# A fused vision tower on one core: two expert tiles gathered by products with tables of ones and zeros, and fillers in the gaps of a solve

## The reference, cut to what matters

```python
scores = jnp.einsum('bsh,he->bse', x, wr) + br
expert_id = jnp.argmax(scores, axis=-1)
h = jax.nn.gelu(jnp.einsum('bsh,ehf->ebsf', x, w1) + b1[:, None, None, :], approximate=False)
y = jnp.einsum('ebsf,efh->ebsh', h, w2) + b2[:, None, None, :]
out = jnp.einsum('ebsh,bse->bsh', y, jax.nn.one_hot(expert_id, E, dtype=x.dtype))
```

## Time and profile before

| | |
|---|---|
| median of 3 runs | 687.46 us (687.45 to 689.64) |
| the profiled execution | 688.33 us, of which the span from first to last instruction is 686.5 |
| TensorE busy | 636.0 us (93% of the span) |
| VectorE, ScalarE, GpSimd busy | 318.3, 278.5, 152.9 us |
| mean granted TensorE clock | 0.968 of full speed |
| the chain that ended last | 77% of the span on TensorE, 13% on VectorE |

### The profile page before, as it was taken

The page is one execution under the profiler, slowest core; times in us unless marked ns, Lnnn a source line. Parts: engine busy times, 40 slices in busy tenths (PEclk is TensorE's granted clock), DMA queues, the critical chain, the costliest instruction groups (busy, mean ns, idle before and its releaser), DMA issues.

```text
span 686.5 us, 20153 instructions
## 1 busy us (share of the span) xinstructions
PE 636.0 (93%) x9158; PEld 467.7 (68%) x9158; DVE 318.3 (46%) x493; ACT 278.5 (41%) x558; POOL 152.9 (22%) x143
## 2 busy tenths in 40 slices
PE   8989879969999995999999988899999999999997
PEld 5646766859999993655665557554999866555553
DVE  0397456510111003757777786599247824311311
ACT  0486441303323231546666652857444532111223
POOL 9400110040111113324554464300333100000000
PEclk9999889889999998999999997999999999999999
DMA  9610045033889912010010201000000160000001
GB/s 320 204 66 4 3 188 205 1 97 114 334 311 315 339 62 75 0 33 23 26 33 23 83 6 62 3 1 0 4 5 4 45 266 1 0 0 1 0 1 47
DMA packets 19700, 56.69 MB, mean 83 GB/s; under 512 B 4079, under 2 KB 12383, under 8 KB 15263
## 3 DMA queue, kind: packets, MB, share of 16 engines
q1 hardware_dynamic: 18559, 52.52, 21.6%
q0 software_dynamic: 1056, 2.89, 1.1%
HBM read 49.62 MB, written 5.78 MB: 81 GB/s over the span
## 4 chain that ended last, share of the span: by engine, by line
PE 77%; DVE 13%; issue 4%; ACT 3%; DMA 2%; POOL 1%; DVEq 0%; ACTq 0%; SPq 0%; POOLq 0%
PE PS L1586 8%; PE PS L1538 8%; PE PS L1549 7%; PE PS L1626 7%; PE PS L1723 6%; PE PS L618 4%; PE PS L576 3%; PE PS L1753 3%; PE PS L1730 3%; PE PS L608 3%; PE PS L597 3%; PE PS L586 3%; PE PS L1397 2%; DVE arena L1892 2%; DVE work L479 2%
## 5 line engine op out<-in xcount | busy, mean ns | idle before, releaser
L1626 PEld LDWEIGHTS PS<-arena 64*49 64x49 f32 x3584 | 50.6, 124 | 36.7 <-issue 22.4
L1586 PE MATMUL PS<-Y,arena 128*128 128x392 f32 x192 | 73.4, 511 | 0.0
L1626 PE MATMUL PS<-arena 64*49 64x48 f32 (+2 forms) x3584 | 57.2, 214 | 10.5 <-DVE arena L1892 5.6
L1269 ACT ACTIVATE arena<-PS,arena 128x128 f32<-128x128 f32 x112 | 32.0, 368 | 81.5 <-PE PS L1538 81.5
L1887 DVE COPY_PREDICATED arena<-msk,PS 128x768 f32<-128x768 int32 x24 | 44.9, 1872 | 27.8 <-PE PS L1626 27.8
L400 POOL TENSOR_TENSOR arena<-arena,work 128x512 f32<-128x512 f32 x20 | 25.4, 1270 | 137.3 <-DVE work L708 137.3
L1538 PEld LDWEIGHTS PS<-arena 128*128 128x128 f32 x448 | 53.6, 197 | 2.4 <-issue 1.8
L1538 PE MATMUL PS<-arena 128*128 128x128 f32 x448 | 53.9, 280 | 1.2 <-DVE arena L1836 1.2
L1170 POOL TENSOR_TENSOR arena<-arena 128x384 f32<-128x384 f32 (+1 forms) x32 | 37.7, 1177 | 76.7 <-PE PS L1626 73.0
L1549 PE MATMUL PS<-arena 128*128 128x256 f32 x224 | 50.5, 379 | 0.0
L1586 PEld LDWEIGHTS PS<-Y,arena 128*128 128x128 f32 x192 | 33.0, 188 | 19.4 <-issue 0.8
(11 more groups left out here) (236 smaller groups left out, 1166.8 us busy)
## 6 DMA issues: line engine op xcount, KB each, us to landing
arena<-in_moe_w SPq DMA_DIRECT2D x28, 1024.0 KB, 6.6
arena<-in_qka_w SPq DMA_DIRECT2D x8, 384.0 KB, 3.0
arena<-in_patches SPq DMA_DIRECT2D x6, 392.0 KB, 5.3
arena<-in_ff_w SPq DMA_DIRECT2D x1, 2048.0 KB, 8.0
arena<-in_ffn_w SPq DMA_DIRECT2D x2, 1024.0 KB, 12.4
by_expert<-arena SPq DMA_DIRECT2D x1, 1799.0 KB, 8.1
arena<-in_moe_b SPq DMA_DIRECT2D x14, 128.0 KB, 7.9
arena<-answers SPq DMA_DIRECT2D x4, 256.0 KB, 3.9
```

The costliest lines, as they stand in the source:

```text
L1269: nc.scalar.activation(G[:, j % 2, f], PS[:, 4 + 2 * (j % 2) + f // 4, (f % 4) * P:(f % 4 + 1) * P], ACT.Gelu, bias=MB1[j % NW][:, f:f + 1 ...
L1586: m = nc.tensor.matmul(bank(i % 3), GW[g % 2][:, k, u // 2], half(Y[:, k], u % 2), start=(k == 0), stop=(k == KT - 1))
L1626: m = nc.tensor.matmul(o, K[r, b, :], v, start=True, stop=True)
```

## The change

A new constant `nth` holds 1 to 128 along the columns. Two operations are added to `route`, behind the row numbers: for tile j (0 and 1), `HOT[j]` is a table of 128 tokens x 8 blocks x 128 places, 1 where the token's number in expert j equals the place and 0 elsewhere. A product of a block of tokens (turned by the product itself) with its table, summed over the eight blocks, gives the tile's rows already turned. `gather(j)` does that for tiles 0 and 1 in place of `turn(j)`, from tokens that still lie in SBUF. The row load of tile 2 is issued first, those of tiles 0 and 1 second (only `ANSWER_OF` of them is still used), then tile 3 alone. The 100 fillers ahead of the tiles become 6. In the first solve, four fillers are put before each of the three last groups of `pe_out`, and five behind it.

```diff
-NT, NX = 14, 6
+NT, NX, NH = 14, 6, 2
...
+        HOT = [at(2304 + 1024 * j, BP * P).rearrange("p (b n) -> p b n", b=BP) for j in range(NH)]
...
-        ROW_LOADS = ((0, 1), (1, 2), (2, 4), (4, 8), (8, 14))
-        rows_load_of = [i for i, (a, b) in enumerate(ROW_LOADS) for _ in range(a, b)]
+        ROW_LOADS = ((NH, NH + 1), (0, NH), (NH + 1, 4), (4, 8), (8, 14))
+        rows_load_of = {j: i for i, (a, b) in enumerate(ROW_LOADS) for j in range(a, b)}
...
         N_CHOSEN, N_OWN, N_PLACED = 5, 8, len(route)
+        route += [lambda j=j: tt(HOT[j], c("nth").unsqueeze(1).broadcast_to([P, BP, P]),
+                                 by_e(number)[:, j].unsqueeze(2).broadcast_to([P, BP, P]), ALU.is_equal) for j in range(NH)]
...
+                if g >= 5:
+                    spin(4, 6)
 
             delta0.pe_out(pe, ahead0)
+            spin(5, 6)
...
+            def gather(j):
+                pe.wait_ge(sc_step, N_PLACED + j + 1)
+                for k in range(KT):
+                    for b in range(BP):
+                        m = nc.tensor.matmul(PS[:, j % 2, k * P:(k + 1) * P], XTOK[:, b, k * P:(k + 1) * P], HOT[j][:, b],
+                                             start=(b == 0), stop=(b == BP - 1))
+                m.then_inc(xt_mm, 1)
...
-            spin(100, 7)
-            turn(0)
+            spin(6, 7)
+            gather(0)
+            gather(1)
             for j in range(NT):
                 up(j)
-                if j + 1 < NT:
+                if 1 < j + 1 < NT and j + 1 >= NH:
                     turn(j + 1)
```

More of the change, by code:

```diff
@@ L55 @@
 for _name, _n in (("mean", P), ("pick", 62), ("ident", P), ("tie", E), ("eps5", 1), ("eps6", 1), ("eps11", 1),
-                  ("ones", P), ("behind_rows", P), ("valid", 1), ("first", 1), ("second", 1), ("pad_rows", B // 2), ("sizes", 6), ("tiles", 6), ("extra", E), ("restart", E * B // 2)):
+                  ("ones", P), ("behind_rows", P), ("valid", 1), ("first", 1), ("second", 1), ("pad_rows", B // 2), ("sizes", 6), ("tiles", 6), ("extra", E), ("restart", E * B // 2), ("nth", P)):
     CON[_name] = (_at, _n)
@@ L2025, in _constants @@
     put("extra", P * (E - 1 - np.arange(E)))
+    put("nth", 1 + r)
     put("restart", np.arange(E * B // 2) % (B // 2) > 0)
```

## The result

The changed kernel took 681.57 us (median of 4 runs, 677.99 to 682.35), the kernel before 688.23 beside it, ratio 0.989 [0.985, 0.993]. It is faster by 1.1%, but not by 12.1 us, and 681.57 lies 2.6 above the top of the range. More executions followed: the changed kernel's 17 have a mean of 679.8 (674.6 to 685.2), those of before that ran beside them, 43 in all, 689.2 (684.7 to 694.9). So the gain is 9.4 us, uncertain by 0.8 (one standard error, from spreads of 3.1 and 2.6 between executions).

What follows compares the result with a forecast made beforehand. TensorE was taken to lose time waiting for rows through HBM before the expert tiles and at half clock after the first solve; 10.1 + 3.0 - 1.0 = 12.1 us gain, so 675.4 us, range 672.5 to 679.

Steps and rivals of the forecast that it cites:

- Slow stretches that follow: Half-clock stretches after the first application, shifted by earlier work: net effect zero, 1.5 us to either side, later ones likewise.
- The start of the sum: The time from which gains were subtracted: 688.33 us for the profiled execution, 0.87 less for the median of 687.46.
- Gain 10.1: From row numbers to tile 2's first products: gathering tiles 0 and 1 by products starts them at 157.6, not 167.74.
- I take 1.0: Allowance of 1.0 us lost because the clock may still be at half when the gathers begin.
- Rival (2): At the gathers: they run at half clock, losing 3.4 us instead of 1.0, total 677.8; chance 12%.
- the prediction's own sign of being wrong: At tiles 0 and 1: the forecast is wrong if the gathers take over 4 us each.
- Net 3.0: End of first solve: fillers hold the clock, 128 application passes take 3.6 us, not 6.71; gain 3.1, loss about 0.1.
- Rival (1): First solve: its fillers don't hold the clock, so 3.1 us less gain, total 678.5; chance 15%.
- The rival of the scatters: After the row numbers: GpSimd scatters wait for VectorE's tables, up to 2.4 us later, total 676.3; chance 8%.
- At nothing: Around the expert tiles: VectorE's delayed routing steps, row loads, expert weights and added constants cost nothing.
- Slower (5): From gather 0 to tile 2: clock stays at half, costing 18 us instead of 1.0, total 692; chance 1%.
- the net of nothing: At the expert tiles: the change nets to nothing because the tiles come to wait for weights; chance 1%.

Runs made afterwards that it cites:

- gather alone: The changed kernel without the fillers in the first solve (gather by products, 6 fillers in place of 100); median 679.89 us, ratio 0.987 to the kernel before.
- the bridge: The changed kernel with 10 fillers instead of 6 ahead of the gathers; medians 677.42 us (0.981 of before) and, timed again, 672.84 us (0.975).
- the waits filled: The changed kernel with 10 fillers ahead of the gathers, 38 in the first application's wait and 56 behind the last tile; 674.67 us, 0.977 of before.
- all filled: The kernel with the waits filled, plus 9 fillers ahead of the fifth group of the second solve; median 675.77 us, 0.979 of before.
- the fillers at the second solve: The changed kernel with 9 more fillers in TensorE's gap ahead of the second solve's fifth group of rows; median 679.58 us.

## Why the prediction failed, point by point

Four traces of the changed kernel and three of before give each stage a mean. The spans' means are 677.6 and 685.4, 7.9 apart:

| stage | before | changed | gain |
|---|---|---|---|
| to the first application | 75.68 | 75.91, 76.31, 75.66, 79.28 | −1.1 |
| to the router scores | 51.88 | 48.42, 48.63, 48.30, 49.15 | 3.3 |
| to the row numbers | 10.45 | 9.08, 10.59, 9.20, 10.31 | 0.7 |
| to tile 2's first products | 29.65 | 22.02, 21.18, 22.16, 19.55 | 8.4 |
| from there to the end | 518.8, 517.9, 516.5 | 524.5, 523.2, 517.5, 519.3 | −3.4 |

**The step that failed: "Slow stretches that follow", "I take zero, with 1.5 to either side, and the same for later ones".** In the trace of the first runs the lead at tile 2 was 12.3, the forecast 12.1, and 5.7 were lost behind it, where the sum has nothing: there half clock covered 34 us, against 17 before. The term has the right cause and the wrong size: the same instructions from tile 2 to the end take 516.5 to 518.8 in three executions of before and 517.5 to 524.5 in four of the changed kernel. The range got 1.5 us for this; one execution differs from the next by up to 7.0. I read three runs within 2.2 us as the spread of the kernel, and that spread is 10.2 us over 43 runs.

**The start of the sum.** 687.46 is the median of three runs; the mean of 43 is 689.2. That is 1.7 of the miss. On the whole: 679.8 − 675.4 = 4.4, of which 1.7 is the start; 12.1 − 9.4 = 2.7 is gain that didn't come. By the table the stages up to tile 2 gained 11.2, 0.9 short; the other 1.8 must lie behind tile 2. The four traces of the changed kernel have 24 us of half clock there in the mean, those of before 15. Whether the earlier work brings that about, or whether it is the scatter between executions, stays open; the three profiled executions of before were themselves 2 us quicker than their kernel's mean, which accounts for more than half of the −3.4.

**"Gain 10.1" was right.** At full clock numbers to tile 2 took 20.03 and 19.55 us (gather alone, and the changed kernel's fourth trace); I had 157.6 − 138.11 = 19.5, counted from the same start (L1020 before). Against 29.65 that is 9.6 and 10.1 gained. The tables take 1.24 each (1.22 said), 64 passes of gathers 7.41 at full clock (7.1 said).

**"I take 1.0" for the clock at the gather: mis-sized.** The two numbers of the first trace: 9.87 us for the gathers, so 2.7 over 7.14. Against the 19.55 without half clock the four traces lost 2.5, 1.6, 2.6 and 0. The mean is 1.7. Rival (2) came in three of four executions, at half to three quarters of its 3.4, and the prediction's own sign of being wrong, gathers of over 4 us each, came too (4.9 in the first trace). I had weighed the gap by the harmless one of 2.2 at 47.3. In the first trace the clock had fallen at 129.8 already, among the router's small products with a wait of 0.48 us for VectorE, so there the gap ahead of the gathers was not the cause of the fall. In the second it fell at 137.5, half a microsecond into the gathers, behind a gap of 1.43 us; in the fourth a gap of 1.38 brought no fall. So the gap's part in it stays open.

**"Net 3.0" for the solve's fillers: mis-sized.** In the first trace the first 128 passes took 3.6 us (75.91 to 79.52) at clock 1.00 as forecast, instead of 6.71. But in the changed kernel's fourth trace the clock fell at 73.0, with the fillers in place, and had fallen already at 49.2, where the code is as before; the bridge's trace shows the same. Measured: 1.4 to 1.8 us in the mean, uncertain by 1.3, so the shortfall is likely and not certain. Over all runs, four of the ten traces with these fillers had such a fall between 69.5 and 84. Rival (1) is thus neither true nor false: it comes true in some executions. I had taken one trace's fall for the kernel's.

**The rival of the scatters.** First scatter 1.02 us behind L1021's start, like before (1.02); it took 1.45 us beside the two tables, against 1.17, the second 0.96 as before. So it was in all fourteen traces: 1.45 or 1.46 in the ten with tables, 1.17 in the four without. A GpSimd instruction that issues a scatter was lengthened by 0.3 us, and no TensorE wait came of it. The rule of the Trainium skill, "SBUF — State Buffer", section "Who interferes with whom", by which the two would exclude each other for the whole instruction, would have set the scatters back by up to 2.4 us; this trace doesn't show that. The same section of the Trainium skill goes on that a `tensor_tensor` was not seen to stall DMAs, which the prediction left out, and on that point the trace agrees but for the 0.3 us.

**What else held.** "At nothing" for loads and weights: no wait for `by_expert`, period 7.24. Slower (5) and the net of nothing didn't come; the longest stretch at half clock in any trace was 17.1 us (69.5 to 86.6, with the waits filled), not 26.

## What to carry to other kernels

A kernel whose granted clock falls here and there has a spread of its own, and one profiled execution shows one draw of it. Before a sum is made to the tenth, look whether the stretches at half clock stand at the same instructions in two or three executions, and give the forecast the spread between executions of the stages that the change only shifts; what the change removes (waits, a trip through HBM) came out to within 0.5 us, and the two terms that hung on the clock were off by a factor of about two. What a filled gap earns depends on what comes behind it: 1 to 2 us in the traces where TensorE had work of its own there, about 0.6 where it soon waited for the next data.

## What the runs showed of the hardware

Two things were not expected. **The same instructions fall to half clock in one execution and not in the next**, in code far from any edit: 49.2 to 59.4 in the changed kernel's fourth trace, 49.4 to 59.6 in the bridge's, 49.6 to 59.9 with all filled, under work that is the same as before; the other eleven traces have none there. With the fall at 73 that came with it, the first application began 3.3 to 5.1 us later than in the mean of the changed kernel's other traces. **And a stage can vary without any fall**: the second application took 96.73 us in one trace of the changed kernel and 99.36 in another, both at clock 1.00, with TensorE busy 94.08 and 95.40, and 100.92 with the fillers at the second solve. The group of line 587 in that stage, in the short one and then in the long one:

```profile
L587 PE MATMUL PS<-arena 49*49 49x64 f32 x512 | 17.4, 216 | 0.0
```

```profile
L587 PE MATMUL PS<-arena 49*49 49x64 f32 x512 | 18.9, 217 | 0.8 <-issue 0.6
```

One product takes as long as before (216 and 217 ns); they start less densely, and the little idleness is put down to nothing that the profile shows. No run separated it, and the cause is open.
